# Attention with its column sums brought back through memory on Pool's queue instead of through TensorE

## The reference, cut to what matters

```python
n = layernorm(x)                                   # over the last axis, eps 1e-5
xd = (n @ W_down).reshape(8, 1024, 16, 16)         # 16 heads of 16
keys, queries = einsum(xd, tokeys) * s, einsum(xd, toqueries) * s      # s = 16 ** -0.25
values = einsum(xd, tovalues)
attn = softmax(einsum('bqhs,bkhs->bhqk', queries, keys), axis=-1)
x = x + einsum('bhqk,bkhs->bqhs', attn, values).reshape(...) @ W_unify + b_unify
```

## Time and profile before

| what | us |
|---|---|
| median of 3 runs | 2889.71 (2889.34 to 2901.28) |
| the profiled execution: time, span | 2896.95, 2895.2 |
| first feed-forward layer, about | 0 to 640 |
| attention, about | 640 to 2260 |
| second feed-forward layer, about | 2260 to 2895 |
| one batch row of attention (start of `times_v`, 1096.61 to 1290.64) | 194.03 |

### The profile page before, as it was taken

How to read it: one execution, slowest core, us unless ns; L and a number is a source line. 1 busy time by engine, 2 the same in 40 slices (tenths; PEclk the granted TensorE clock), 3 DMA queues, 4 the chain that set the end, 5 groups by cost and what they waited for, 6 DMA issues and landing times. The chain is left out here.

```text
span 2895.2 us, 48611 instructions
## 1 busy us (share of the span) xinstructions
PE 2705.7 (93%) x17009; PEld 1644.3 (57%) x17009; DVE 2145.9 (74%) x3552; ACT 1821.3 (63%) x3409; POOL 599.8 (21%) x562
## 2 busy tenths in 40 slices
PE   5899999867999999999999999999999589999997
PEld 3799999863334334333343343433433368999886
DVE  6555456747899898998998988989895665554574
ACT  5344556632777776777777767777777444444564
POOL 3355114521100100101001001010000235521353
PEclk9899999986999999999999999999999789999998
DMA  5211113414123132131231321312310512111341
GB/s 172 66 44 44 58 45 106 133 60 75 30 50 75 33 61 54 39 62 36 50 75 33 60 55 39 62 37 50 60 28 5 173 30 80 44 44 45 102 133 63
DMA packets 164529, 181.69 MB, mean 63 GB/s; under 512 B 38472, under 2 KB 133904, under 8 KB 164368
## 3 DMA queue, kind: packets, MB, share of 16 engines
q1 hardware_dynamic: 156176, 169.03, 24.0%
q0 software_dynamic: 8192, 10.57, 1.2%
HBM read 97.51 MB, written 31.54 MB: 45 GB/s over the span
## 5 line engine op out<-in xcount | busy, mean ns | idle before, releaser
L1457 ACT ACTIVATE at_ex<-at_pd 128x512 f32<-128x512 f32 x2048 | 1084.7, 600 | 383.7 <-PE at_pd L1360 379.2
L1521 DVE TENSOR_REDUCE at_mxc<-at_pb 128x2 f32<-128x1024 f32 x1024 | 1219.0, 1219 | 120.8 <-PE at_pb L1349 113.8
L768 DVE TENSOR_TENSOR f_ml_hl<-f_ml_h,f_ml_hh 128x512 fp32r<-128x512 f32 (+1 forms) x384 | 287.8, 751 | 422.7 <-ACT f_ml_hh L844 421.5
L1360 PE MATMUL at_pd<-at_qa,at_ka 50*128 50x512 f32 x2048 | 583.6, 469 | 3.9 <-ACT at_ex L1457 3.2
L1360 PEld LDWEIGHTS at_pd<-at_qa,at_ka 50*128 50x128 f32 x2048 | 266.6, 185 | 538.4 <-issue 349.2
L1369 PE MATMUL at_po<-at_ex,at_va 128*32 128x512 f32 x4096 | 548.8, 608 | 0.2 <-ACT at_ex L1457 0.2
L841 ACT ACTIVATE f_ml_h<-f_ml_pL,b1T 128x512 f32<-128x512 f32 (+1 forms) x384 | 243.8, 635 | 457.9 <-PE f_ml_pL L895 446.3
L1349 PE MATMUL at_pb<-at_ka,at_qa 48*128 48x512 f32 x2048 | 433.1, 450 | 24.7 <-DVE at_mxc L1521 16.5
L910 PE MATMUL f_ml_pA<-f_wh,f_ml_hh 128*128 128x256 f32 (+1 forms) x1408 | 410.4, 291 | 3.7 <-DVE f_ml_hl L768 3.7
L912 PE MATMUL f_ml_pA<-f_wl,f_ml_hh 128*128 128x256 f32 (+1 forms) x1408 | 402.5, 286 | 0.0
L913 PE MATMUL f_ml_pA<-f_wh,f_ml_hl 128*128 128x256 f32 (+1 forms) x1408 | 402.5, 286 | 0.0
(11 more groups left out here) (128 smaller groups left out, 2636.6 us busy)
## 6 DMA issues: line engine op xcount, KB each, us to landing
f_wraw<-in_L_ffn_w SPq DMA_DIRECT2D x128, 256.0 KB, 2.8
at_qa<-at_parts SPq DMA_DIRECT2D x384, 64.0 KB, 2.4
at_ka<-at_parts SPq DMA_DIRECT2D x384, 64.0 KB, 2.4
f_ro_xr<-in_L_attn_x SPq DMA_DIRECT2D x16, 512.0 KB, 3.9
f_ml_xr<-in_L_attn_x SPq DMA_DIRECT2D x16, 512.0 KB, 4.2
x<-f_ml_yo SPq DMA_DIRECT2D x16, 512.0 KB, 4.0
at_xr<-x SPq DMA_DIRECT2D x16, 512.0 KB, 5.1
at_xres<-x SPq DMA_DIRECT2D x8, 1024.0 KB
```

The costliest lines, as they stand in the source:

```text
L768: eng.tensor_tensor(hl[h % RING][:, 0:w], h32[h % 2][:, 0:w], hh[h % RING][:, 0:w].bitcast(F32), ALU.subtract).then_inc(s_lo.sem, 1)
L1360: eng.matmul(pd[n % RING][:, :], ka[g][rows, p, kt * P:(kt + 1) * P], qa[g][rows, qh, p, :], start=True, stop=True).then_inc(s_full.sem, 1)
L1457: eng.activation(ex[t % 2][:, j, :], pd[n % RING][:, :], ACT.Exp).then_inc(s_free[n % RING].sem, 1)
L1521: eng.tensor_reduce(mxc[:, t // NT, kh, t % NT::NT], pb[kh][:, :].rearrange("p (e k) -> p e k", e=2), AX.X, ALU.max, negate=True).then_inc ...
```

## The change

The turn through PE is given up. ACT copies `po` to `os_` (in the last step of a half, after its exponentials). Pool then issues, for each half, five DMAs: `os_` to a buffer in memory (`oscr`, 256 KB); from there the totals into `tot` (128x16, 8 KB) and the sums into half a tile of `aT`, already with the output columns on partitions (64 partitions, 128 KB); DVE takes the reciprocal of `tot`; Pool sends it to memory (`rscr`, 8 KB) and reads it back spread over the partitions of each head (`den`, 64 partitions, 128 KB). After each second unit Pool multiplies `aT` by `den`, 128x512. The tasks `f` and `aT` are gone from PE, ACT and DVE; `ao` and `rec` too. The tasks `u` move: to t = 2, 4, 10, 11 of the next batch row's first unit, and for the last batch row's first half to t = 14, 15 of its last unit. LayerNorm is applied on Pool (except before the loop), the statistics move to t = 2, 4, 10, 11, `xT` to 7, 8, 13, 14, `xd` to 12 and to 1, 2, 3 of the second unit. A `qk` bank is copied once, by ACT, to `xT`, and Pool makes its two parts there, as it does for the keys. Some semaphores are joined. The residual's bias is added at t = 14 instead of 8.

```diff
         def side_at(g, t, prev, last):
-            table = {1: ("f", 1), 9: ("f", 0)}
...
-                table.update(zip((2, 3, 5, 6), OUT(1)))
-            if g == 3:
-                table.update(zip((10, 11, 13, 14), OUT(0)))
+                table.update(zip((2, 4, 10, 11), OUT(0) + OUT(1)))
+            if g == 3 and last:
+                table.update(zip((14, 15), OUT(0)))
             if g == 0 and not last:
-                table.update(zip((7, 8, 10, 11, 13, 14), XT + XD))
+                table.update(zip((7, 8, 12, 13, 14), [*XT[:2], XD[0], *XT[2:]]))
             if g == 1 and not last:
-                table.update(zip((2, 3, 5, 6, 7, 8), XD[-2:] + QK))
+                table.update(zip((1, 2, 3, 5, 6, 7, 8), XD[1:] + QK))
...
# SP
-                    eng.wait_ge(s_kp.sem, s_kp.at(2 * len(XD) * b + len(XD) * (c + 1)))
+                    eng.wait_ge(s_kp.sem, s_kp.at(PARTS * b + 2 * len(XD) + len(QK) * (c + 1)))
...
# ACT
+            def values_out(b, g, t):
+                eng.wait_ge(s_pv.sem, s_pv.at(ST * unit(b, g) + t + 1))
+                if half(b, g, t // NT):
+                    eng.wait_ge(s_os.sem, s_os.at(16 * half(b, g, t // NT)))
+                eng.activation(os_[:, :], po[:, :], ACT.Copy).then_inc(s_o.sem, 1)
...
+                    if t % NT == NT - 1:
+                        values_out(b, g, t)
...
# DVE
+            def reciprocals(b, g, qh):
+                eng.wait_ge(s_td.sem, s_td.at(16 * (half(b, g, qh) + 1)))
+                eng.reciprocal(tot[:, :], tot[:, :]).then_inc(s_rc.sem, 1)
+            STATS_AT = {2: (0, FIRST), 4: (0, SECOND), 10: (1, FIRST), 11: (1, SECOND)}
...
+                    if t == NT + 4:
+                        reciprocals(b, g, 0)
+                    if t == 4 and (b or g):
+                        reciprocals(*before(b, g), 1)
+                    if g == 0 and not last and t in STATS_AT:
+                        stats(b + 1, *STATS_AT[t])
...
# Pool
+            def sums_out(b, g, qh):
+                eng.wait_ge(s_o.sem, s_o.at(half(b, g, qh) + 1))
+                eng.dma_start(oscr[g, qh, :, :, :].rearrange("j r q -> (j r) q"), os_[:, :]).then_inc(s_os.sem, 16)
+            def sums_in(ring, b, g, qh, read):
+                eng.wait_ge(s_os.sem, s_os.at(16 * (half(b, g, qh) + 1)))
+                eng.dma_start(tot[:, :], oscr[g, qh, :, HS, :].rearrange("j (x y) -> j x y", y=HS)).then_inc(s_td.sem, 16)
...
+                eng.dma_start(aT[r0:r0 + HS * GH, qh, g // 2, :], oscr[g, qh, :, 0:HS, :]).then_inc(s_nd.sem, 16)
+            def totals_out(b, g, qh):
+                eng.wait_ge(s_rc.sem, s_rc.at(2 + half(b, g, qh) + 1))
+                eng.dma_start(rscr[g, qh, :, :].rearrange("j (x y) -> (j x) y", y=HS), tot[:, :]).then_inc(s_rs.sem, 16)
+            def totals_in(b, g, qh):
+                eng.wait_ge(s_rs.sem, s_rs.at(16 * (half(b, g, qh) + 1)))
...
+                eng.dma_start(den[r0:r0 + HS * GH, qh, :], src).then_inc(s_nd.sem, 16)
+            def divide(b, g, qh):
+                eng.wait_ge(s_nd.sem, s_nd.at(16 * 2 * (half(b, g, qh) + 1)))
+                if g % 2:
+                    eng.tensor_tensor(aT[:, qh, g // 2, :], aT[:, qh, g // 2, :], den[:, qh, :],
+                                      ALU.mult).then_inc(s_dv.sem, 1)
...
+                    if past and t % NT == 0:
+                        sums_out(*past)
+                    if past and t % NT == 1:
+                        sums_in(self.ring, *past, self.read[past[2]])
+                    if past and t % NT == 5:
+                        totals_out(*past)
+                    if past and t % NT == 6:
+                        totals_in(*past)
+                    if g == 0 and not last and t in (5, 12):
+                        normalize(self.ring, b + 1, t // 8, side)
+                    if past and t % NT == 7:
+                        divide(*past)
```

More of the change, by code:

```diff
@@ L1158, in attention @@
              (3, 9), (3, 13), (0, 1), (0, 5), (0, 7), (0, 9), (0, 13), (1, 1)))}
-        splits = lambda task: task[0] == "qk"
+        landed = lambda g, p: s_ld[0] if (g, p) == (0, 0) else s_ld[1 + g]
+        loads = lambda g, b: (ULOADS if g else ULOADS // 2) * 2 * 16 * b
         half = lambda b, g, qh: 2 * unit(b, g) + qh
@@ L1162, in attention @@
         next_unit = lambda b, g: (b, g + 1) if g < 3 else (b + 1, 0)
+        before = lambda b, g: (b, g - 1) if g else (b - 1, 3)
         half_ahead = lambda b, g, t: (b, g, 1) if t < NT else (*next_unit(b, g), 0)
@@ L1180, in __init__ @@
                 self.ring = do.ring = Ring()
-                self.ns, self.side, self.ready = 0, None, None
+                self.side, self.ready = None, None
                 sides = [self.place(task, 0, 0, 0) for task in XT + XD + QK[:2] + V + QK[2:]]
@@ L1194, in __init__ @@
                         self.phase(do, b, b % 2, g, prev=b > 0, last=b == NBAT - 1)
-                do.end([self.place(task, NBAT - 1, 1, 3) for task in [("f", 1)] + OUT(1)])
+                do.end([self.place(task, NBAT - 1, 1, 3) for task in OUT(1)])
             def place(self, task, b, par, g):
                 n = self.ring.take()
-                a = Place(task, b, par, g, n, self.ns, self.side)
+                a = Place(task, b, par, g, n, self.side)
                 self.side = n
-                self.ns += splits(task)
                 return a
@@ L1218, in phase @@
                         a = self.place(task, b + 1, 1 - par, g)
-                    elif task == ("f", 1):
-                        a = self.place(task, *((b, par, g - 1) if g > 0 else (b - 1, 1 - par, 3)))
-                    elif task and task[0] in ("aT", "u") and g == 0:
+                    elif task and task[0] == "u" and g == 0:
                         a = self.place(task, b - 1, 1 - par, g)
@@ L1227, in phase, with units_landed @@
                     do.step(b, par, g, t, coming, tiles, done, a, side, ahead, last)
+        def units_landed(eng, b, c):
+            for g, p in ((0, 0), (0, 1), (1, 0)) if c == 0 else ((2, 0), (3, 0)):
+                eng.wait_ge(landed(g, p).sem, landed(g, p).at(loads(g, b)))
         block = ctx.enter_context(nc.Block())
@@ L1232, in _ @@
         def _(eng):
-            for s in (*s_xr, *(x for two in s_ld for x in two), *s_mr, s_ms, s_xl, *s_st):
+            for s in (*s_xr, *s_ld, *s_mr, s_ms, s_xl, *s_st):
                 s.open(eng)
@@ L1451, in _ @@
         def _(eng):
-            for s in (s_hi, *s_free):
+            for s in (s_o, *s_free):
                 s.open(eng)
@@ L1515, in _ @@
             norm.open_vector(eng)
-            for s in (s_xn, s_mx, s_nm, s_o, s_rc):
+            for s in (s_xn, s_mx, s_nm, s_rc):
                 s.open(eng)
@@ L1682, in step @@
                 def step(self, b, par, g, t, coming, tiles, done, a, side, ahead, last):
-                    if g == 0 and not last and t in (1, 5):
-                        norm.pow_step(eng, 2 * (b + 1) + t // 4, 4)
-                    if a and a.kind == "xd":
-                        key_parts(self.ring, a)
-                    if g == 2 and t == 8:
+                    past = (b, g, 0) if t >= NT else (*before(b, g), 1) if b or g else None
+                    if past and t % NT == 0:
[10 more added lines that the diff above has]
+                        divide(*past)
+                    if a and a.kind in ("xd", "qk"):
+                        two_parts(self.ring, a)
+                    if a and a.kind == "u":
+                        self.read[a.at[0]] = a.n
+                    if g == 2 and t == 14:
                         eng.wait_ge(s_xl.sem, s_xl.at(16 * (8 + b + 1)))
```

201 lines of the change are left out of this document (86 added, 115 removed).

## The result

The changed kernel takes 2905.7 us in the median of 8 runs, the kernel before 2894.4 in 8 runs (three of them those of the prediction). The ratio is 1.0044, with a 95% interval of 1.0028 to 1.0061: slower by less than half a percent, where a fall from 2889.7 to 2857, 1.1% faster, was forecast.

A forecast was written before the change was run, and what follows sets the result against it. PE sets the pace, a plain step bound by the loop PE, exponential, PE. Terms -45.6 - 5.6 + 5.9 + 4.0 + 9.0 = -32.3 us take the median from 2889.7 to 2857; 8-in-10 range 2842 to 2890.

The forecast's parts named there:

- LayerNorm on Pool: At a batch row's beginning: `xn` ready 5.6 us after `times_v`, before PE asks, so nothing; at most 1.1 each.
- rival 3: At a batch row's beginning: `xn` late at its upper bound, +7.7 us, 2865; chance 0.08.
- PE's transposes: In attention's steps: 93 steps lose the transposes of `f` and `aT`, 0.49 us each: -45.6 us.
- The stall at a batch row's beginning: DVE, overloaded in a batch row's first steps, loses work: 0.94 us saved in each of 6 batch rows, -5.6.
- ACT's copy: Behind a half, copying from PSUM delays ACT's next exponential: 49 halves times 0.12 us, +5.9, at most 9.8.
- Pool's chain: In the steady state: two DMA trips of 3.2 us, 6.4 allowed, before DVE's reciprocal; 7.7 us behind it; costs nothing.
- Rival 1: DVE waits for `tot` at t = 4 and 12; trips of 7.2 us would give about 2974; chance 0.15.
- The start: Before the loop: SP's first `load_head` also needs two query tasks' parts from Pool: +4.0 us.
- The end: From last `times_v` to last addition: four trips of 3.2 us make 14.3 us into 23.3, +9.0.
- Rival 2: Pool holds up DVE's joining of maxima, +0.79 us for one in two of 47 halves: +19, 2876; chance 0.15.

The follow-up runs named there:

- the last experiment: Copy out of PSUM on DVE instead of ACT, against the changed kernel with `xT` later and both start and end mended: 2850.8 us, ratio 0.9866.

## Why the prediction was wrong, point by point

**The step that failed** is "LayerNorm on Pool". I bounded a 128x256 application between half the cast and half the subtraction of 128x512, 0.30 to 0.64 us, and took the lower end: `xn` ready 5.6 us after `times_v`, PE's question at 5.9 and 6.9, so nothing. The instruction took 1.21 us, above the upper bound. `xn` was ready 8.8 us after instead, and PE asked at 6.0 and 7.4. It is a size that was off, in a mechanism that stood in the text with its place (rival 3); but its price then had a cap of 1.1 us for a batch row, and moving `xT` away from it gave back 6.5. The cap was wrong twice: by the duration, and because it counted only the waits. Of the 7.1 us of longer steps, 4.7 are waits (32.8 / 7) and 0.4 is DVE's late statistics at t = 6, which is no part of this step and is still there in the run with `xT` later. The other 2 are products at the lower clock behind the second wait: step 13 is 0.8 us longer than 3.10 and its wait together (the four transposes alone 0.43), and step 14 is 1.45 longer (its `times_v`, which starts at 1147.78, alone 0.86). At t = 7 some 0.15 of the wait was hidden.

For all seven batch rows that is 45.6 us where the forecast had nothing, and it accounts for the miss. The forecast was -32.3; with 45.6 added it is +13.3. Attention grew by 12.2 us in the traces, and the medians of 8 by 11.3. That the two agree so closely is partly luck, as the slow steps in the last unit of the kernel before flatter the change by 3.6.

**PE's transposes** cost what was said. In the changed kernel t = 1 and 9 of the last two units, and t = 10 and 11 of the fourth, take 2.60 to 2.62 us, where 3.10 stood before. With `xT` later, whole batch rows take 188.2 us, where 187 to 188 was forecast.

**The stall at a batch row's beginning** went, as forecast: the plain step 3 behind `u` takes 2.61. A smaller one appeared, 0.41 at t = 6, where reciprocal and statistics stand in plain steps, so that about half of the 0.94 was gained. The run of LayerNorm alone in the kernel before shows most of the old stall was DVE's applications (3.43 to 2.79).

**ACT's copy** was sized at 0.12 us a step; it is 0.09. The lines around one such copy:

```profile
1248.68 1.07 PE L1369 MATMUL at_po<-at_ex,at_va 128*32 128x512 f32 x8
...
1249.81 0.60 ACT L1458 ACTIVATE at_os<-at_po 128x512 f32<-128x512 f32 x1
...
1250.30 2.06 ACT L1452 ACTIVATE at_ex<-at_pd 128x512 f32<-128x512 f32 x4
...
1250.94 0.18 PEld L1360 LDWEIGHTS at_pd<-at_qa,at_ka 50*128 50x128 f32 x1 [0.40 <-ACT at_ex L1452]
...
1251.37 1.07 PE L1369 MATMUL at_po<-at_ex,at_va 128*32 128x512 f32 x8
```

The exponentials start 1.62 after `times_v` instead of 1.53, the fourth product's weights wait 0.40 instead of 0.31, and the step takes 2.69. The loop of PE and ACT passes the 0.09 on unchanged.

**Pool's chain** was judged rightly where the sum rests on it: the trips to `tot` took 2.6 and 2.2 us at the end, far below 6.4, and DVE waited nowhere in the steady state. Its second part was not. From the reciprocal to the end of the multiplication 7.7 us were forecast; from the end of the reciprocal at 1113.64 it took 15.0, to 1128.68. The issue of `den` stands behind the four applications on Pool and began at 1120.97, when they ended, and the multiplication could start at 1127.39. The `u` that needs it began at 1129.84, 1.2 us later; in six batch rows of the changed kernel this margin was 0.2 to 3.5 us, and in the last experiment it was used up three times. So LayerNorm on Pool, at that place, also nearly made the chain late. The issues landed after, from the changed kernel's page and DMA view (KB each, median us):

```profile
at_oscr<-at_os POOLq DMA_DIRECT2D x64, 256.0 KB, 2.4
...
at_aT<-at_oscr POOLq DMA_DIRECT2D x64, 128.0 KB, 4.1
at_den<-at_rscr POOLq DMA_DIRECT2D x64, 128.0 KB, 4.2
...
at_tot<-at_oscr POOLq DMA_DIRECT2D x64, 8.0 KB, 2.2
at_rscr<-at_tot POOLq DMA_DIRECT2D x64, 8.0 KB, 2.3
```

Rival 1, a late `tot`, was out. The Trainium skill's formula (DMA: Bandwidth & Descriptors, Anatomy of one DMA: SWDGE path), 2.0 us plus bytes / 436e3, gives by estimate 2.6 us for the 256 KB store, 2.0 for 8 KB and 2.3 for 128 KB. The trace agrees for the first two (2.4, 2.2 and 2.3) and not for the last (4.1 and 4.2).

**The start** was +4.0 forecast, +3.6 to SP's first load measured, and undoing it gave it back. **The end** was +9.0 forecast from 23.3 us; it is 22.7, +8.4. The sum of four trips, 11.5 us, was near the 12.8 taken.

**Rival 2**, Pool holding up DVE, is real and stayed small. In either kernel 7 of the 64 joinings take 0.95 to 0.97 us, each of them beside a subtraction on Pool, and none of the other 57 is beside one or longer than 0.18. The joining of maxima in the changed kernel:

```profile
L1523 DVE TENSOR_TENSOR at_nm<-at_mxc x64: 174/176/968, 695.5 to 2210.8; 128x16 f32<-128x16 f32 x64
```

Median and maximum are those of the earlier trace rows, with four times Pool's work in the batch row. Pool's long operations lie elsewhere in the step list.

**The prediction's form.** The range of 2842 to 2890 left out a case that was named. Rival 3 got 0.08 and no upper price beyond the nearest rows, although no row showed a Pool operation of that kind (two operations with a scalar for each partition). The bound from other kinds was treated as a bound of this one.

## What to carry to other kernels

- When work moves to an engine on which that kind of instruction has no row, the neighbours' durations are no upper bound. Work out the duration at which the plan fails (here 4 x d + 1.2 had to be under 2.5 to 3.5 us, so d under 0.3 to 0.6) and ask how sure d is; there was almost no margin, and one step of the table was worth 34 us.
- A side task's place is part of its price. The same slow application was a gain of 5 to 8 us with four steps of lead and a loss of 45.6 with one or two. A wait of 3 us on PE cost more than 3 us here, as the products behind it ran at the lower clock.
- Round trips that a long loop hides stand bare at its two ends. Four trips at the end and two tasks at the start cost 12 us here. Undone there alone, the start gave back 4.1 and the end 6.4.

## What the runs showed of the hardware

- Pool's `tensor_scalar` of 128x256 float32 with a scalar for each partition takes 0.91 us with one operation and 1.21 with two. A cast of twice the size takes 0.61. DVE does the one with two operations in 0.40.
- DVE's reciprocal of 64x512 from PSUM takes 3.36 us, a multiplication of the same shape 0.69; 128x16 takes 0.25.
- On Pool's queue a load of 64 partitions with 2 KB each lands after 4.1 us, a store of 128 partitions with 2 KB each after 2.4. Each plain issue keeps Pool 0.57 to 0.78 us.
- DVE operations on two tiles, or on a tile and two scalars for each partition, were held up beside Pool's subtraction of two 128x512 tiles: 0.95 to 0.97 us instead of 0.18 for the joining of the maxima (7 of 7), 1.04 instead of 0.40 for the application of LayerNorm (6 of 7, the other 0.86). The subtraction itself kept to 1.27 to 1.29.
- Before `xT`'s second wait PE ran score products and side products at 2.4 GHz; then it did nothing for 2.96 us, and the granted clock was 0.57 over 8 us, most of them at 1.2 GHz. In the last unit, where the products for the maxima have ended and PE has only those for the exponentials and `times_v`, some profiled executions fell to the lower level and some did not: steps of 4.07 instead of 2.61, none in the changed kernel's, one in the kernel before and one with the copy on DVE, two with `xT` later, six with the start undone. There they and the longer step behind them took 11.7 us.
